# Expert slots without the old rows: the gathers add the experts' results to the rows in place

## What is computed

```python
# x: 4096 rows of 128, E = 8 experts, C = 4096 // 8 = 512 slots each
idx = argmax(softmax(x @ Wr + br))                    # one expert for each row
pos = cumsum(one_hot(idx), axis=0)                    # the row's place in its expert
mask = one_hot(idx) * (pos < C)                       # a row beyond the capacity is dropped
gate = max(probs) * mask
expert_in = dispatch of gate * layernorm(x)           # (E, C, D)
eo = relu(expert_in @ W1 + b1) @ W2 + b2
x = x + gate * eo[expert, pos]                        # a dropped row keeps x
```

## Time and profile before

| | us |
|---|---|
| median of 3 executions | 690.64 |
| the profiled execution | 693.44 |
| its span (first to last instruction) | 691.4 |
| last scatter issued | 568.5 |
| expert loads issued from | 570.7 |
| first gather | 599.7 |
| last gather issued | 645.5 |

### The profile page before, as it was taken

How to read it: one execution, slowest core, us unless ns; L and a number is a source line. 1 busy time by engine, 2 the same in 40 slices (tenths; PEclk the granted TensorE clock), 3 DMA queues, 4 the chain that set the end, 5 groups by cost and what they waited for, 6 DMA issues and landing times. The chain is left out here.

```text
span 691.4 us, 13756 instructions
## 1 busy us (share of the span) xinstructions
PE 545.4 (79%) x4905; PEld 261.3 (38%) x4905; DVE 501.0 (72%) x1038; ACT 421.1 (61%) x746; POOL 230.4 (33%) x325
## 2 busy tenths in 40 slices
PE   3774789899999889899889899888588309866884
PEld 2451233332333333333332333332188307645573
DVE  4999779789888888799897788890077413436687
ACT  1970278678878778777778778678523104133551
POOL 2562012212212224313315212216117470288611
PEclk9996599999999999999999999999965558967598
DMA  7389445476335154203142114010043247210022
GB/s 178 94 169 295 89 109 131 124 190 183 100 61 100 37 107 86 52 7 76 27 80 55 29 30 86 15 37 10 9 111 114 62 123 276 97 26 22 12 62 62
DMA packets 66756, 61.11 MB, mean 88 GB/s; under 512 B 12114, under 2 KB 56051, under 8 KB 66677
## 3 DMA queue, kind: packets, MB, share of 16 engines
q1 hardware_dynamic: 58000, 53.97, 31.1%
q10 hardware_dynamic: 6128, 2.90, 1.6%
q0 software_dynamic: 2560, 3.38, 1.6%
HBM read 33.03 MB, written 29.85 MB: 91 GB/s over the span
## 5 line engine op out<-in xcount | busy, mean ns | idle before, releaser
L897 DVE TENSOR_REDUCE neg_max<-bank 128x2 f32<-128x1024 f32 (+2 forms) x320 | 342.0, 1113 | 62.3 <-PE bank L810 58.8
L928 ACT ACTIVATE probs<-ring 128x512 f32<-128x512 f32 (+4 forms) x485 | 301.9, 677 | 73.0 <-PE ring L838 61.3
L838 PE MATMUL ring<-q_operand,k_operand 56*128 56x512 bf16 (+3 forms) x768 | 163.1, 332 | 18.9 <-ACT probs L928 15.1
L859 PE MATMUL sums<-probs,v_all 128*9 128x512 f32 (+3 forms) x1536 | 162.7, 496 | 5.7 <-POOL probs L965 4.3
L965 POOL TENSOR_SCALAR_AFFINE_SELECT probs<-probs 128x512 f32<-128x512 f32 x128 | 80.6, 634 | 219.1 <-ACT probs L928 218.4
L810 PE MATMUL bank<-k_operand,q_operand 54*128 54x512 bf16 (+3 forms) x768 | 143.0, 341 | 7.0 <-DVE v_all L595 5.3
L838 PEld LDWEIGHTS ring<-q_operand,k_operand 56*128 56x128 bf16 x768 | 50.5, 94 | 147.5 <-ACT probs L928 102.9
L804 PE MATMUL bank<-masks 64*128 64x128 bf16 (+2 forms) x768 | 71.4, 225 | 6.6 <-DVE neg_max L897 5.3
L810 PEld LDWEIGHTS bank<-k_operand,q_operand 54*128 54x128 bf16 x768 | 46.0, 97 | 23.9 <-DVE neg_max L897 12.1
L804 PEld LDWEIGHTS bank<-masks 64*128 64x128 bf16 x768 | 36.2, 96 | 42.9 <-DVE neg_max L897 30.9
L1360 POOL DMA_INDIRECT early<-expert_out,back x32 | 32.5, 1016 | 39.2 <-issue 39.2
(11 more groups left out here) (192 smaller groups left out, 670.4 us busy)
## 6 DMA issues: line engine op xcount, KB each, us to landing
q_operand<-q_rows SPq DMA_DIRECT2D x64, 96.0 KB, 3.7
k_operand<-k_rows SPq DMA_DIRECT2D x32, 192.0 KB, 4.5
q_rows<-early SPq DMA_DIRECT2D x36, 128.0 KB, 2.4
k_rows<-early SPq DMA_DIRECT2D x36, 128.0 KB, 2.4
expert_rows<-fill SPq DMA_DIRECT2D x16, 257.0 KB, 3.9
rows<-expert_rows SPq DMA_DIRECT2D x8, 514.0 KB, 6.6
weighted_sums<-osum SPq DMA_DIRECT2D x128, 18.0 KB
sums_in<-in_L_attn_x SPq DMA_DIRECT2D x4, 512.0 KB, 7.3
```

The source lines that it names most:

```text
L838: last = nc.tensor.matmul(psS[:, bank, w * j:w * j + w], k_op[rows, buf, p, P * kb:P * kb + P], q_op[rows, buf, c, p, q0:q0 + w], start=Tr ...
L859: last = nc.tensor.matmul(psO[32 * i:32 * i + HD + 1, q0:q0 + w], v_all[:, n, kb, i, :], probs[:, u % NPROBS, i // 2, i % 2, 0:w], start=u ...
L897: nc.vector.tensor_reduce(neg_max[:, n % 2, slot, kc, :, pairs[0]:pairs[-1] + 1, t % CH], src, AX.X, ALU.max, negate=True).then_inc(a_read, 1)
L928: nc.scalar.activation(dst, src, ACT.Exp).then_inc(ring_read, 1)
```

## The change

The constants are moved so that the gated row and the gate are the first 129 columns (`SENT`) of a block in `rows`, and the old row the last 128. Only the first 129 columns, 516 bytes, are sent; `expert_rows`, the cleared tile `fill` and its constant are that wide. The expert loads go into a new tile `es` of that width. VectorE's last step for an expert is `tensor_scalar` yb * gate with no addend. `expert_out` gets one more row, of zeros, stored by a ninth DMA of SyncE, for which the first fetch also waits. `back` is limited to that row's index, so that a dropped row fetches zeros, and the gathers add to `x2` in the transfer (`compute_op=ALU.add`) where they had overwritten it.

```diff
--- before.py
+++ after.py
@@ -36,7 +36,7 @@
 SROWS = AROWS + MAXROWS
 FILL = -3.0e38
 NOWHERE = 1 << 20
-XG, X1, GATE, ROW = 0, D, 2 * D, 2 * D + 1
+XG, GATE, SENT, X1, ROW = 0, D, D + 1, D + 1, 2 * D + 1
 
 
 def bf16_bits(a):
@@ -71,7 +71,7 @@
     sel = np.zeros((H, CHUNKS, CHUNKS, P), np.float32)
     for j in range(CHUNKS):
         sel[np.arange(P) % H, j, j, np.arange(P)] = 1.0
-    fill = np.zeros((P, 2, ROW), np.uint32)
+    fill = np.zeros((P, 2, SENT), np.uint32)
     return {
         "c_qrows": bf16_bits(qrows.reshape(2, BIASROWS, GH * QC * 2 * CW)),
         "c_krows": bf16_bits(krows),
@@ -81,7 +81,7 @@
         "c_sel": sel.reshape(P, CHUNKS * P),
         "c_incl": bf16_bits(np.arange(P)[:, None] <= np.arange(P)[None, :]),
         "c_ones": bf16_bits(np.ones((P, P))),
-        "c_fill": fill.reshape(P, 2 * ROW),
+        "c_fill": fill.reshape(P, 2 * SENT),
         "c_samet": (at[:, None] == at[None, :]).astype(np.float32),
         "c_rank": np.tile((E - np.arange(E)).astype(np.float32), (P, 1)),
     }
@@ -305,9 +305,9 @@
         q_dram = nc.dram_tensor("q_rows", (NG, 2, 2, NPROD, HD, S), BF16).ap()
         k_dram = nc.dram_tensor("k_rows", (NG, 2, 2, NPROD, HD, S), BF16).ap()
         o_dram = nc.dram_tensor("weighted_sums", (NG, GH, HD + 1, S), F32).ap()
-        slots_dram = nc.dram_tensor("expert_rows", (E * CAP, ROW), F32).ap()
+        slots_dram = nc.dram_tensor("expert_rows", (E * CAP, SENT), F32).ap()
         x1_dram = nc.dram_tensor("x1_rows", (B * S, D), F32).ap()
-        y_dram = nc.dram_tensor("expert_out", (E * CAP, D), F32).ap()
+        y_dram = nc.dram_tensor("expert_out", (E * CAP + 1, D), F32).ap()
         rden_dram = nc.dram_tensor("reciprocals", (EARLY, H, S), F32).ap()
 
 
@@ -319,7 +319,7 @@
         bqc, bkc = sb("bqc", [P, 1]), sb("bkc", [P, 1])
         bvb = sb("bvb", [P, D])
         rows = sb("rows", [P, TILES, ROW])
-        fill = sb("fill", [P, 2, ROW], U32)
+        fill = sb("fill", [P, 2, SENT], U32)
 
 
         early = sb("early", [P, 9 * S])
@@ -1047,7 +1047,7 @@
         later_stages(nc, ctx, sb, sem, w, dict(
             rows=rows, ot=ot, den=den, ident=ident, half_pow=half_pow, banks=half + [b0, b1_, b2_, b3],
             wts_in=wts_in, o_in=o_in, xb_ready=xb_ready, rden_ready=rden_ready, n_later=NLATER,
-            slots_clear=slots_clear, slots_dram=slots_dram, x1_dram=x1_dram, y_dram=y_dram, router=router, place_counts=place_counts,
+            slots_clear=slots_clear, slots_dram=slots_dram, x1_dram=x1_dram, y_dram=y_dram, fill=fill, router=router, place_counts=place_counts,
             at_ready=at_ready, x1_ready=x1_ready, x1_out=x1_out, ve2_ready=ve2_ready, pw2_ready=pw2_ready, scales_ready=scales_ready,
             lg_ready=lg_ready, ex_ready=ex_ready, hot_ready=hot_ready, slot_ready=slot_ready, row_ready=row_ready,
             scattered=scattered), r, out)
@@ -1258,7 +1258,7 @@
     router, place_counts = shared["router"], shared["place_counts"]
     back = sb("back", [P, TILES], U32)
 
-    es = rows[:, :, :].rearrange("p (e a) f -> p e a f", a=CH)
+    es = sb("es", [P, E, CH, SENT])
     xgt, hid = sb("xgt", [P, 2, CW]), sb("hid", [P, 2, CW])
     yb = sb("yb", [P, 2, CH, D])
     ye = sb("ye", [P, E, CH, D])
@@ -1321,6 +1321,7 @@
         for e in range(E):
             sp.dma_start(es[:, e, :, :].rearrange("p a f -> p (a f)"),
                          slots_dram[CAP * e:CAP * e + CAP, :].rearrange("(p a) f -> p (a f)", a=CH)).then_inc(es_in[e], 16)
+        sp.dma_start(y_dram[E * CAP:E * CAP + 1, :], shared["fill"][0:1, 0, 0:D].bitcast(F32)).then_inc(y_out, 16)
         for e in range(E):
             sp.wait_ge(ye_ready, e + 1)
             sp.dma_start(y_dram[CAP * e:CAP * e + CAP, :].rearrange("(p a) d -> p a d", a=CH), ye[:, e, :, :]).then_inc(y_out, 16)
@@ -1347,20 +1348,20 @@
             else:
                 pool.wait_ge(row_by_dve, u - (TILES - CH) + 1)
             nc.gpsimd.indirect_dma_start(
-                out=slots_dram, out_offset=bass.IndirectOffsetOnAxis(ap=slot[:, u:u + 1], axis=0), in_=rows[:, u, :],
+                out=slots_dram, out_offset=bass.IndirectOffsetOnAxis(ap=slot[:, u:u + 1], axis=0), in_=rows[:, u, 0:SENT],
                 in_offset=None, bounds_check=E * CAP - 1, oob_is_err=False).then_inc(scattered, 16)
 
         def fetch(j):
 
             if j == 0:
                 pool.wait_ge(back_ready, 1)
-                pool.wait_ge(y_out, 16 * E)
+                pool.wait_ge(y_out, 16 * (E + 1))
             pool.wait_ge(x2_in[j], 16 * B)
             for u in range(CH * j, CH * j + CH):
                 nc.gpsimd.indirect_dma_start(
                     out=x2[:, u, :], out_offset=None, in_=y_dram,
                     in_offset=bass.IndirectOffsetOnAxis(ap=back[:, u:u + 1], axis=0),
-                    bounds_check=E * CAP - 1, oob_is_err=False).then_inc(y_in[j], 16)
+                    bounds_check=E * CAP, oob_is_err=True, compute_op=ALU.add).then_inc(y_in[j], 16)
 
         def root(z, j):
             pool.wait_ge(ve_ready[z], j + 1)
@@ -1462,7 +1463,7 @@
                     nc.vector.tensor_scalar(rows[:, u, XG:XG + D], rows[:, u, X1:X1 + D], nt2[:, 0, u:u + 1], nt2[:, 1, u:u + 1],
                                             ALU.mult, ALU.add).then_inc(row_by_dve, 1)
         dve.wait_ge(back_psum, 1)
-        nc.vector.tensor_copy(back[:, :], psBack[:, 0:TILES]).then_inc(back_ready, 1)
+        nc.vector.tensor_scalar(back[:, :], psBack[:, 0:TILES], float(E * CAP), None, ALU.min).then_inc(back_ready, 1)
 
 
         nc.vector.memset(xe[:, :, :, D:D + 1], 1.0)
@@ -1472,8 +1473,7 @@
                                     b2b[:, e:e + 1, :].to_broadcast([P, CH, D]), ALU.add).then_inc(yb_ready, 1)
             dve.wait_ge(yb_ready, e + 1)
             for a in range(CH):
-                last = nc.vector.scalar_tensor_tensor(ye[:, e, a, :], yb[:, e % 2, a, :], es[:, e, a, GATE:GATE + 1],
-                                                      es[:, e, a, X1:X1 + D], ALU.mult, ALU.add)
+                last = nc.vector.tensor_scalar(ye[:, e, a, :], yb[:, e % 2, a, :], es[:, e, a, GATE:GATE + 1], None, ALU.mult)
             last.then_inc(ye_ready, 1)
```

## The result

The changed kernel takes 708.74 us (median of 4 executions, 704.22 to 712.3) against 692.33 us for the kernel before (4 executions, with one more than shown at the start). The ratio is 1.0228, 95% interval 1.0150 to 1.0307; a second measurement on another chip gave 1.0244 (1.0182 to 1.0306). So the change costs some 16 us, and the forecast of 690.5 us, with a range up to 706, was wrong; from the 690.64 us that it started from, 16.4 us more would be 707.0. The profiled execution took 712.3 us, its span is 710.0 us.

What follows compares the result with a forecast made beforehand. The prediction took GpSimd's time for each gather in the last stage as what stands on the path many times over. Its terms summed to -0.1 us from a median of 690.64, giving 690.5 us, range 684 to 706 us.

Steps and rivals of the forecast that it cites:

- The gathers: Last stage, GpSimd: the 32 adding gathers cost 0 us more, with up to +0.5 us each kept for the range.
- rival (a): Last stage, GpSimd: each gather takes 1.5 instead of 1.0 us, 10 to 16 us more, say 703 us; chance 0.27.
- The lower bound: Last stage: 20 gathers stand ahead of the one on the chain, so 20 x 0.5 = 10 us more, 700.5 us.
- The transfers: Last stage, DMA engines: an adding gather's transfer takes about 0.65 us instead of 0.17, under the 1.27 us period, hidden.
- rival (b): Last stage: the adding transfers become the bound, over 1.27 us for each gather; at 2.6 us, 732 us; chance 0.10.
- The landing: Last stage: the gathers' data land later by 0.5 us or so, hidden by 2.2 us of slack.
- doubled reads: Last stage, GpSimd: a gather takes up to 2.0 us, 20 to 32 us more, 710 to 723 us; chance 0.04.
- The expert loads: Start of the experts: loads halve to 2.1 MB, but idle products set TensorE's start; 0 us, bound -0.3.
- VectorE's tail: End of the experts: VectorE's last steps as `tensor_scalar` gain 0.04 to about 0.8 us; taken as -0.1 us.
- The clears: Under the attention: 16 clears become half as large, their landing awaited only 340 us later; 0 us.
- the scatters: Ahead of the experts, GpSimd: 32 scatters, their time not set by row size; 0 to -0.3 us, taken as 0.
- the limiting of `back`: VectorE: it replaces a copy long before its use; 0 us.

Runs made afterwards that it cites:

- e8: The changed kernel with adding gathers that move 256 instead of 512 bytes for each row; 701.0 us, beside 683.67 us for the kernel before.
- e3: The changed kernel with adding gathers in chunks 5 to 7 only (12 of 32), the rest overwriting; 695.99 us, ratio 1.0070 to the kernel before.
- e4: The changed kernel with adding gathers in chunks 0 to 4 only (20 of 32), the rest overwriting; 699.40 us, ratio 1.0106 to the kernel before.
- e1: The changed kernel with gathers that overwrite instead of adding, dropped rows still moved; 688.84 us, ratio 0.9974 to the kernel before.
- e5: The changed kernel with overwriting gathers that skip dropped rows, as in the kernel before; 681.43 us, ratio 0.9976 to the kernel before.
- e2: The kernel before with a GpSimd memset of 256 columns behind each of the 32 gathers; 693.61 us, ratio 1.0023 to the kernel before.
- e15: The changed kernel with plain gathers into the space of `ye`, VectorE adding, and four instead of six idle products on TensorE; 692.32 us, ratio 0.9974 to the kernel before.

## Why the prediction was wrong, point by point

**The gathers: the step that failed.** The prediction said: "Time seems to go by 128 indices, and those stay. [...] I take 0, because the two measured forms agree so well". The first half is right as far as e8 goes: bytes don't count (the number of indices no run varied). The second does not follow from it. That the time does not go by bytes says nothing of what is done for one row, and the two forms that agreed, plain gather and plain scatter, both read one place and write one. The form at hand has the old row to read as well. The rows bore the comparison only on the axis along which they differed. Measured, the term is 0.56 us for each of 32, where I took 0 and held 0.5 for the upper bound. So rival (a) was what happened, a gather's instruction half as long again on the engine that bounds the stage, and nearly at its price: it gave 703, at most 706.5 us, from a median of 690.64; measured were 16.4 us over the kernel before. Its reason, that the work goes by the places that are read and written, fits the 0.56 us but is not shown.

**How much of it reaches the end.** Rival (a) had 20 to 32 gathers on the path. It is nearly all 32: the last twelve added 6.6 us where 12 x 0.56 is 6.7 (e3), the first twenty 9.1 of 11.2 (e4), and all together 17.5 of 17.9 over e1. The lower bound came from reading the chain of waits as if all that it does not pass were free, while the earlier trace rows showed five roots behind the last gather. The plain versions show how little one chain says here. In e1 it leaves GpSimd already at the root of 608.88 us, behind the eighth gather, and goes on over TensorE; in e5, whose first and last gather lie as far apart within 0.3 us, it stays on GpSimd to the last gather. So the two ways must be nearly equally long, and a longer gather counts almost from the start. Some slack of this kind may be why e2's 6 us came through only in part; that is not shown.

**The transfers.** The estimate of 0.65 us of each DMA engine for an adding gather is close. In the first 6.4 us of the changed kernel's last stage its queue is busy for 19.5% of 16 engines, 1.25 us each for 327 packets or 2.3 gathers, 0.55 us a gather:

```profile
q0 software_dynamic: 5632, 3.23, 3.0%
...
q0 software_dynamic: 327, 0.15, 19.5%
```

That is below the 1.87 us from gather to gather, as said, so rival (b) fell. The landing was to be later by 0.5 us or so; it went from 2.4 us to 3.6, of which some 0.5 come with the dropped rows and 0.6 with the longer instruction. The bytes of this queue hardly change (3.38 to 3.23 MB), but the packets more than double. The Trainium skill ("DMA: Bandwidth & Descriptors", "Rules for kernel authors"), named there, says that an accumulating DMA reads its destination and writes it later; no run here shows that this costs time at the landing. What the Trainium skill says beside rival (a) ("GPSIMD Engine Reference", "4. When to use GPSIMD") has one core write the reads' list and another the writes'. Its doubled reads would have allowed 1.0 us more for each gather; measured are 0.56, so what goes by the reads is only part of the instruction, or the writes' list set the old time. No run here tells these apart.

**The expert loads: right.** They land sooner, at the soonest after 2.7 us instead of 3.7, and the zero row's DMA is issued 0.5 us behind the last of them, as said:

```profile
L1322 SPq DMA_DIRECT2D es<-expert_rows x8: 348/432/433, 575.0 to 578.2; - x8
...
DMA to landing us min/median/max: 2.7/4.1/4.8
...
L1324 SPq DMA_DIRECT2D expert_out<-fill x1: 376/376/376, 578.7 to 578.7; - x1
```

And the first transposes still follow the idle products at once:

```profile
575.04 4.89 PE L1642 MATMUL ring<-sel,ident 128*128 128x256 f32 x12 [14.36 <-DMA expert_rows<-rows,early]
579.76 0.49 PE L1653 MATMUL bank<-ident,es 128*128 128x128 f32 x3
```

The products take 4.89 instead of 5.24 us, at a granted clock of 0.58 instead of 0.54 in that stretch, which is the same work (2.8 us at full clock in both); the loads had no part in the start, as e15 shows.

**VectorE's tail: right in place, too small in size.** The new operation is neither like the 341 ns nor like the 227 ns of the earlier trace rows:

```profile
L1476 DVE TENSOR_SCALAR ye<-yb,es x32: 279/281/289, 585.2 to 600.0; 128x128 f32<-128x128 f32 x32
```

It takes 281 ns. TensorE's last product ends at 598.15 us and VectorE at 600.26, 2.11 us later instead of 2.65, so the tail gave 0.5 us where I took 0.1:

```profile
596.05 2.10 PE L1667 MATMUL ring<-w,hid 128*128 128x128 f32 x16
...
597.87 0.88 DVE L1476 TENSOR_SCALAR ye<-yb,es 128x128 f32<-128x128 f32 x4
...
598.66 0.68 DVE L1472 TENSOR_TENSOR yb<-ring,b2b 128x512 f32<-128x512 f32 x1
599.38 0.88 DVE L1476 TENSOR_SCALAR ye<-yb,es 128x128 f32<-128x128 f32 x4
```

The Trainium skill's rule ("VectorE: DVE Perf Modes", "Mode 2×_2P"), a one-source fp32 operation at two results a cycle, would by my reckoning have given about 0.8 us. The number lies between the rule's and the row's. e1 and e5, the change without the adding, each stand some 0.25% or 1.7 us under the kernel before, e1 within its interval and e5 just beyond it; no run tells how much of that is the tail.

**The rest.** The clears, the scatters (986 ns, as 985 before, for half the bytes) and the limiting of `back` cost nothing, as said.

## What to carry to other kernels

When the engine that issues the indirect transfers is the fullest of its stage, count its time for each transfer, not the bytes. Here halving 4.2 MB of loads gave about nothing, and 0.56 us more in each of 32 gathers gave 16 us. An addition put into the transfer was paid by that engine in every instruction, while the same addition on an engine that stands idle for half of the stage cost 1.4 us for all, and not more than 3.6. And if two forms of an instruction take equally long, that bounds a third form only as far as it differs along the same axis; where it does more for each element, the forecast should lie inside the range and not at its lower end. How much of a longer instruction reaches the end is asked of runs that lengthen a part of them, as e3 and e4 do, since the chain of one profile can lie beside a second one that is nearly as long.

## What the runs showed of the hardware that was not expected

- An adding gather of 128 rows keeps GpSimd for 1560 ns, a plain one 1000 to 1012, a casting one 1004. The 1560 are the same for 256 and for 512 bytes a row.
- Casting and adding gathers show 144 packets each on the queue, plain ones 32, with no effect of their number to be seen on the instruction's time (the cast has them too, at 1004 ns) or on the landing (2.9 us cast, 3.0 plain; 3.6 adding, where the issue is 0.56 longer).
- A dropped index that is skipped and one that fetches a shared row of zeros take the same time of GpSimd within 12 ns a gather, though the latter moves nearly twice the rows; it lands 0.5 us later (3.0 us instead of 2.5).
- A `tensor_scalar` of 128x128 fp32 took 341 ns with two per-partition operands, 281 ns with one and 227 ns with a constant and no other.
